# A gather table that ends in 127 copies of its last row, with each partition clamped to a copy of its own

## The reference, cut to what matters

```python
N, DIM, B, L, LAYERS = 12501, 128, 512, 50, 2
h = acc = emb                                             # [N, 128]
for _ in range(LAYERS):                                   # 150000 edges
    h = jax.ops.segment_sum(adj_val[:, None] * h[adj_col], adj_row, num_segments=N)
    acc = acc + h
graph_item_embs = acc / (LAYERS + 1)
combined = graph_item_embs[items] + item_features[items]  # items: [512, 50]
seq_hidden = jnp.take_along_axis(combined, alias_inputs[..., None], axis=1)
...                                                       # attention over the 50 items
sess_emb = jnp.sum(beta * seq_hidden, axis=1)
select = W_K * _l2norm(sess_emb)
scores = select @ _l2norm(graph_item_embs).T              # [512, 12501]
```

## Time and profile before

| what | value |
|---|---|
| time, median of 3 runs | 4186.96 us (4185.63 to 4187.47) |
| profiled execution, span | 6020.2 us |
| profiled execution, a time of its own beside the span | none given |
| part 1, sort and set-up, in the span | 0 to 773 us |
| part 2, layers, in the span | 773 to 3236 and 3263 to 5569 us |
| part 3, `combined` and norms | 5569 to 5597 us |
| part 4, sessions and scores | 5597 to 6020 us |
| POOL gathers from `combined` | 200, 947 ns each (median) |

### The profile page before, as it was taken

One profiled execution on the slowest core, in us unless ns is written; L12 is line 12 of the kernel. 1 busy time (PEld: TensorE's weight loads), 2 busy tenths in 40 slices (PEclk: granted clock), 3 DMA queues, 4 the chain that ended last, 5 costly groups with the idle time before them and its releaser, 6 DMA issues.

```text
span 6020.2 us, 68764 instructions
## 1 busy us (share of the span) xinstructions
PE 3070.2 (51%) x9778; PEld 1849.5 (31%) x9778; DVE 3014.4 (50%) x7257; ACT 866.4 (14%) x3005; POOL 2890.1 (48%) x2965
## 2 busy tenths in 40 slices
PE   5988744444444444444444444444444444445578
PEld 3777622222222222222222222222222222222344
DVE  8999754444444444444444444444444444445455
ACT  2998800000000000000000000000000000000543
POOL 1666654444444444444445454454454454455561
PEclk8888866666666666666666666666666666666689
DMA  0000011111111111111114111111111111112454
GB/s 25 4 3 3 3 48 33 32 31 32 32 31 33 33 34 33 34 33 31 32 32 120 34 37 35 33 37 36 32 37 35 33 37 35 34 36 80 79 84 139
DMA packets 162229, 235.35 MB, mean 39 GB/s; under 512 B 67554, under 2 KB 107776, under 8 KB 161952
## 3 DMA queue, kind: packets, MB, share of 16 engines
q0 software_dynamic: 92896, 171.14, 12.4%
q1 hardware_dynamic: 54132, 58.90, 3.0%
q10 hardware_dynamic: 15052, 3.83, 0.3%
HBM read 192.69 MB, written 41.01 MB: 39 GB/s over the span
## 4 chain that ended last, share of the span: by engine, by line
ACTq 49%; issue 32%; DVE 7%; PE 6%; ACT 3%; another core or an unknown queue 2%; POOL 1%; DMA 0%; DVEq 0%; SPq 0%; POOLq 0%
ACTq L686 43%; ACTq L682 5%; ACT big L644 2%; PE bank L1520 1%; PE bank L1382 1%; POOL sorted_edges L542 1%; DVE stage L944 1%; PE bank L1548 1%; DVE acc L1167 1%; DVE big L888 1%; PE bank L1507 1%; DVE ring L896 0%; PE bank L1482 0%; DVE big L904 0%
## 5 line engine op out<-in xcount | busy, mean ns | idle before, releaser
L1444 PE MATMUL bank<-ring 128*128 128x256 f32 x4976 | 2105.7, 558 | 2135.8 <-DVE ring L1118 1194.1
L1444 PEld LDWEIGHTS bank<-ring 128*128 128x128 f32 x4976 | 1147.7, 263 | 3071.0 <-DVE ring L1118 1662.5
L574 POOL DMA_INDIRECT ring<-in_L_rec_emb,cring x1195 | 1134.9, 950 | 1336.2 <-ACT cring L662 978.9
L1167 DVE TENSOR_TENSOR acc<-acc,bank 128x256 f32 x2488 | 1029.6, 414 | 1481.3 <-remote 1131.6
L1118 DVE TENSOR_SCALAR ring<-bank,mlo,mval 128x256 f32<-128x256 f32 x2488 | 1343.5, 540 | 742.4 <-DMA ring<-in_L_rec_emb 523.1
L574 POOL DMA_INDIRECT ring<-table,cring x1195 | 1130.2, 946 | 1202.8 <-PE bank L1444 795.7
L644 ACT ACTIVATE big<-big 128x68 f32<-128x68 bf16 x1764 | 557.7, 405 | 1.2 <-issue 1.2
L1382 PE MATMUL bank<-big,ring 128*128 128x136 f32 x2352 | 430.8, 328 | 75.5 <-issue 20.8
L542 POOL DMA_INDIRECT sorted_edges<-moved,block_to x313 | 397.2, 1269 | 100.3 <-issue 100.0
L1382 PEld LDWEIGHTS bank<-big,ring 128*128 128x128 f32 x2352 | 356.8, 219 | 147.6 <-ACT big L644 83.2
L660 ACT COPY mlo<-ring 128x24 f32 (+1 forms) x104 | 21.7, 209 | 2415.0 <-issue 2381.6
(11 more groups left out here) (213 smaller groups left out, 1700.7 us busy)
## 6 DMA issues: line engine op xcount, KB each, us to landing
ring<-in_L_rec_emb SPq DMA_DIRECT2D x3136, 0.5 KB
ring<-in_L_rec_emb ACTq DMA_DIRECT2D x3136, 0.5 KB
ring<-table ACTq DMA_DIRECT2D x3136, 0.5 KB
ring<-table SPq DMA_DIRECT2D x3136, 0.5 KB
scores<-stage SPq DMA_DIRECT2D x48, 512.0 KB
ring<-in_L_rec_emb,cring POOLq DMA_INDIRECT x1195
ring<-table,cring POOLq DMA_INDIRECT x1195
table<-big SPq DMA_DIRECT2D x7, 896.0 KB, 9.1
```

The source lines that it names most:

```text
L574: pool.indirect_dma_start(msg[:, s, :], None, source, bass.IndirectOffsetOnAxis(cring[:, s:s + 1], 0)).then_inc(s_g[s], 16)
L1167: add = dve.tensor_tensor(acc[:, bass.ds(off, BUCKET)], acc[:, bass.ds(off, BUCKET)], bank[u % PR][:, 0:BUCKET], ALU.add)
L1444: pe.matmul(bank[u % PR][:, 0:BUCKET], msg[:, h * T + u, :], onehot[:, u % SR, :], start=True, stop=True).then_inc(s_mm[u % M], 1)
```

## The change

The table `combined` gets N + 127 rows in place of 12544. The rows N to N + 126 are copies of row N - 1 = 12500. The clamp of line 1128 takes min(x, N - 1 + p) on partition p, then max(., 0), in place of max(x, 0), then min(., N - 1): a clamped item of partition 0 reads row 12500, that of partition 127 reads row 12627. The bound comes from a new [128, 1] tile `own_last`, which POOL fills with an iota early in the program. The last of SP's seven DMAs is cut into three, and the two waits on `s_cw` wait for nine.

```diff
+    COPIES = P - 1
-        combined = nc.dram_tensor("combined", [ROWS, D], F32).ap()
+        combined = nc.dram_tensor("combined", [N + COPIES, D], F32).ap()
...
-                sp.dma_start(tab[1][:, a:b, :], ring_rows[:, a:b, :]).then_inc(s_cw, 16)
+                if b <= emb_full:
+                    sp.dma_start(tab[1][:, a:b, :], ring_rows[:, a:b, :]).then_inc(s_cw, 16)
+                    continue
+                sp.dma_start(tab[1][:, a:emb_full, :], ring_rows[:, a:emb_full, :]).then_inc(s_cw, 16)
+                sp.dma_start(tab[1][0:emb_rest, emb_full, :], ring_rows[0:emb_rest, emb_full, :]).then_inc(s_cw, 16)
+                sp.dma_start(combined[N:N + COPIES, :].rearrange("(o n) d -> o n d", o=1),
+                             ring_rows[emb_rest - 1:emb_rest, emb_full, :].unsqueeze(1).broadcast_to([1, COPIES, D])
+                             ).then_inc(s_cw, 16)
...
-            pool.wait_ge(s_lat, 2)
+            pool.iota(own_last[:, :], [[0, 1]], base=N - 1, channel_multiplier=1,
+                      allow_small_or_imprecise_dtypes=True).then_inc(s_lat, 1)
+            pool.wait_ge(s_lat, 3)
...
-            pool.wait_ge(s_cw, 16 * (NB // GRP))
+            pool.wait_ge(s_cw, 16 * (NB // GRP + 2))
...
-            dve.wait_ge(s_lat, 3)
+            dve.wait_ge(s_lat, 4)
...
-                link(dve.tensor_scalar(it_n[:, :, :], it_f[:, :, :], 0.0, float(N - 1), ALU.max, ALU.min))
+                link(dve.tensor_scalar(it_n[:, :, :], it_f[:, :, :], own_last[:, 0:1], 0.0, ALU.min, ALU.max))
...
-            dve.wait_ge(s_cw, 16 * (NB // GRP))
+            dve.wait_ge(s_cw, 16 * (NB // GRP + 2))
```

More of the change, by code:

```diff
@@ L246, in recommender_program @@
         startc = sb("startc", [P, 1])
+        own_last = sb("own_last", [P, 1])
         tile_off = sb("tile_off", [1, NT], I32)
@@ L407, in recommender_program @@
         emb_rest = N - emb_full * P
-        tab = [t.rearrange("(g p) d -> p g d", p=P) for t in (table1, combined)]
+        tab = [t[0:ROWS, :].rearrange("(g p) d -> p g d", p=P) for t in (table1, combined)]
+        assert N + COPIES >= ROWS and emb_full == ROWS // P - 1 and 0 < emb_rest < P
         big_rows = big[:, :].rearrange("p (g d) -> p g d", d=D)
```

## The result

The changed kernel takes 4152.07 us (4147.14 to 4154.12, 4 runs) against 4186.30 us for the kernel before beside it (4185.03 to 4187.47). The ratio is 0.992, interval 0.9908 to 0.9932: faster by 0.8%, where I had forecast no measurable change and 4190 us. Measured again beside each other later, the two took 4150.63 and 4175.19 us, a ratio of 0.994 (0.9923 to 0.9956). The gain of these two pairs is 34 and 25 us. The kernel before took 4174.0 to 4186.3 us over the five comparisons of this document; the changed one was timed in two of them only.

A forecast was written before the change was run, and what follows sets the result against it. The timed kernel was taken to spend most of its time at POOL's pace of issuing gathers. The added write's +4.0 us and the hot row's -0.6 make +3.4 on 4187.0, so 4190 us, "the same"; range 4150 to 4201.

The forecast's parts named there:

- What bounds the kernel: Whole kernel: most time goes at POOL's pace of issuing gathers in the layers, 1.25 us each; the change acts afterwards.
- The 52 us: Outside the layers: time by which 2988 us of gather issuing exceeds 2936, taken to be missing elsewhere in the timed run.
- The added write: Table write before the session gathers: 127 copies on one engine and 85 rows delay POOL's start, +4.0 us passing in full.
- rival C: Table write: the 127 copies of one row are slow, 101 ns each or 12.8 us, giving 4199.5 us; chance 15%.
- The iota and the clamp: POOL's iota, covered by a 63.8 us wait, and the clamp at the layer's start, covered by POOL's pace: 0.
- The removed hot row: Session gathers: without the repeated row, only the landing of batch 0's last gather gets shorter on the path, -0.6 us.
- Rival B: Session gathers beside score writes: DMA engines are the bound, 1.28 us per gather; some 15 us to win, 4172 us; chance 23%.
- rival A: Session gathers: the halts are real and caused by the hot row; 56 us, 4131 us if all goes; chance 12%.
- the halts: While POOL gathers without pause: PE, ACT and DVE stop for 4.5 us at a time in the first profile.

The follow-up runs named there:

- the second profile: The kernel before, unchanged, run and profiled once more: 4174.30 us against 4176.29, ratio 0.9998; profile span 4169.1 us.
- The copies alone: The changed kernel with the old clamp, so the 127 copies are written but clamped items still read row 12500: 4179.75 us, ratio 1.0006 against the kernel before.
- the profile with two rows: The kernel before, no copies written, partitions 0 to 63 clamping to row 12500 and 64 to 127 to 12499: 4157.64 us against 4182.51, ratio 0.9942.
- thin writes: The kernel before with each score write taking 16 of the 128 rows: 4149.67 us, ratio 0.9938 against the kernel before.

## Why the prediction was wrong

**What bounds the kernel, and which stretch it is.** Right, though the profile was a poor one. That the layers go at POOL's pace is what the unstretched profile of the changed kernel says: in 770:3760 POOL is busy with gathers for 2236 us and spends 704 us between them. The 52 us that I found missing outside the layers was the recording too: the tail that I read as 424 us lasts 371.7 in the second profile, 424 - 52. But I didn't go on to read the tail in that light.

**The added write, +4.0 us.** Right in kind, a little too large: POOL waits 3.3 us longer. The copies do run on one engine, and the price of one, 28.9 ns, came out as 24, so rival C, at 101 ns, is out. That the later start passes in full to the end isn't shown. The copies alone made the kernel 0.06% slower, 2.5 us, with an interval that includes nothing. Beside the spread they can't be seen: 0.9945 without copies, 0.994 with them, each to within 0.0016 (7 us).

**The iota and the clamp, 0.** Right. The iota takes 0.65 us under the same cover, and the new clamp, from DVE's line, is no dearer than the old (0.30):

```profile
L1140 DVE TENSOR_SCALAR it_n<-it_f,own_last x1: 324/324/324, 762.6 to 762.6; 128x200 f32<-128x200 f32 x1
```

**The removed hot row, -0.6 us: this is the step that failed.** "All other landings have slack as long as POOL or the arithmetic sets the pace." In w = 1 and 2 neither set it; the DMA engines did. In its place the runs showed -22.6 us there. The gathers' landings of batch 2 had no slack, which cost PE its waits in w = 1, and neither had the landings of the score writes, which share the engines with the gathers and held up DVE and ACT in w = 2. The term itself, for batch 0, was small as forecast: from the first gather to w = 0 the three profiles with the hot row take 68.2 to 69.0 us and those without 65.9 to 67.3.

**Rival B is what happened,** with 23% and 15 us where the profiles show 22.6. The range, 4150 to 4201, holds the measured time, but its lower end came from halves of rival A's gain, which wasn't there. B's sum had the right terms and the wrong divisor. I divided by the 27 gathers that POOL issued in the window; the queue moved 827 / 32 = 25.8 of them, which makes 1.33 us and not 1.28. In the unstretched profile the same sum is (0.812 + 0.182) x 40 / 27 = 1.47 us of engine time per gather moved, clearly above POOL's 1.25 us; divided by the 33 issued it would be 1.20, and seem to fit. What I held against B was wrong. That the stretch w = 1 does more arithmetic and so leaves 1.6 us per gather came from dividing 79.9 us of a stretched profile by 50 gathers. POOL runs ahead, and asks for a gather every 1.25 us whatever the arithmetic does. And a share near 1 was the limit after all: with 99.4% the writes moved 2.98 MB in 40 us and the gathers 1.76, with 48.9% it was 4.47 and 2.10.

**Rival A** had the halts as the row's doing. They are absent from the second profile of the same kernel., the same halts with random rows, was the right witness.

That the first pair differed by 34 us and the later comparisons of full kernels by 23 to 25 is not explained. One thing on record bears on it. A gather of `combined` takes POOL 947 ns (median) in the first profile of the kernel before, and 947 in the profile with two rows, whose chip made both kernels slow: 4182.51 and 4157.64 us, about 7 more than elsewhere. In all other profiles, the first one of the changed kernel among them, it is 944 or 945. So part of the 34 us may be a slower POOL under the kernel before alone. There is no unstretched profile of the kernel before at 4186 us that could tell.

## What to carry to other kernels

When many partitions gather with a clamped or padded index, look at the DMA time per packet of those gathers beside that of random ones: if it is several times higher, two to four different rows were enough here. Whether it is worth anything is decided by whoever shares the DMA engines at that moment, so add up the engine time of all queues, divide it by the work that they moved and not by the work issued, compare that with the issuer's pace, and count the waits for the other queue's landings as well as those for the gathers. And if a profile is much longer than the timed run, take a second one before believing its slack.

## What was not expected of the hardware

- With reads of one 512-byte row by 94 of 128 partitions asked for every 1.25 us (38 GB/s from one row), a packet took 603 ns beside the score writes, with all engines full; with 47 reads (19 GB/s) 165 ns, with 24 reads 135 ns. The jump lies between the first two, and nothing here says whether a channel of the memory or something ahead of it sets it.
- With the engines full both queues lost: from issue to landing it took 16.2 us for a score write (2.8 after the change) and 13.2 us for a gather (4.4 with thin writes), while POOL kept issuing at 1.25 us. The writes moved a third less than after the change, the gathers a sixth less.
- 128 writes of one row out of one partition, on at least 12 engines at once, took 200 ns each in the microsecond read; on one engine 127 of them took 27 ns each.
- One kernel gave a profile of 6020.2 us and one of 4169.1. The short one agrees with the timed runs to 0.2%.
